# Linear attention's opening: the first head's taps and convolution in halves of the tokens, and the first two steps in an order of their own

## The reference

```python
q = hidden @ Wq; k = hidden @ Wk; v = hidden @ Wv
beta = sigmoid(hidden @ Wb + bb); gate = silu(hidden @ Wg)
q = layernorm(silu(causal_dwconv(q, qconv_w, qconv_b)))   # 4 taps
k = layernorm(silu(causal_dwconv(k, kconv_w, kconv_b)))
# for each token: S = (1 - b) * S + b * v k^T ;  o = S q
out = (o * gate) @ Wo
```

## Time and profile before

| | us |
|---|---|
| median of 3 runs | 1080.46 (1079.77 to 1082.92) |
| the profiled execution, its own time | 1079.62 |
| span of that execution, first to last instruction | 1077.7 |
| first projection of head 0 on TensorE | starts at 390.75 |
| `rows_q(2)`, the first TensorE work of loop step 3 | starts at 459.37 |
| one step after that (`rows_q(3)`) | starts at 481.41 |

### The profile page before, as it was taken

The page is one execution under the profiler, slowest core; times in us unless marked ns, Lnnn a source line. Parts: engine busy times, 40 slices in busy tenths (PEclk is TensorE's granted clock), DMA queues, the critical chain, the costliest instruction groups (busy, mean ns, idle before and its releaser), DMA issues. The chain is left out here.

```text
span 1077.7 us, 19332 instructions
## 1 busy us (share of the span) xinstructions
PE 1020.7 (95%) x6893; PEld 807.8 (75%) x6893; DVE 780.1 (72%) x1645; ACT 676.2 (63%) x1229; POOL 500.4 (46%) x441
## 2 busy tenths in 40 slices
PE   7899999999999986899999999999799999999997
PEld 4333333467888885799899888999699778888997
DVE  5789999646677747889998999989567465333843
ACT  3488888766554447887788787887445353333454
POOL 3252320114079642777767777676406000437443
PEclk9999999999999999899999999999899999999999
DMA  4434443233134203322231122210001113555100
GB/s 96 86 69 65 72 65 62 61 96 102 60 108 109 38 6 114 106 96 64 70 103 64 55 65 87 86 67 23 7 30 40 46 48 100 149 157 170 60 21 20
DMA packets 80794, 79.31 MB, mean 74 GB/s; under 512 B 29384, under 2 KB 67740, under 8 KB 80700
## 3 DMA queue, kind: packets, MB, share of 16 engines
q1 hardware_dynamic: 79968, 77.14, 27.2%
q10 hardware_dynamic: 732, 0.95, 0.3%
HBM read 65.51 MB, written 1.28 MB: 62 GB/s over the span
## 5 line engine op out<-in xcount | busy, mean ns | idle before, releaser
L733 ACT ACTIVATE attn_probs<-attn_rows_k 128x512 f32<-128x512 f32 x256 | 138.9, 595 | 24.4 <-PE attn_rows_k L579 21.2
L579 PE MATMUL attn_rows_k<-attn_q_stack,attn_k_stack 50*128 50x512 f32 x256 | 93.9, 446 | 0.0
L2933 DVE TENSOR_TENSOR late_mids<-late_mids,late_bank 128x512 f32<-128x512 f32 (+1 forms) x50 | 34.4, 688 | 78.3 <-PE late_bank L67 75.3
L842 DVE TENSOR_REDUCE attn_row_max<-attn_rows_q 128x1 f32<-128x1024 f32 x62 | 75.9, 1224 | 11.4 <-PE attn_rows_q L563 5.4
L842 DVE TENSOR_REDUCE attn_row_max<-s_sum 128x1 f32<-128x1024 f32 x62 | 75.7, 1220 | 11.0 <-PE attn_rows_q L563 5.2
L592 PE MATMUL attn_ctx<-attn_probs,attn_v 128*32 128x256 f32 x1024 | 81.5, 391 | 1.6
L65 PE MATMUL late_bank<-net_x_part_low,late_w_T 128*128 128x512 f32 (+1 forms) x192 | 77.9, 406 | 0.0
L66 PE MATMUL late_bank<-net_x_part_low,late_w_T 128*128 128x512 f32 (+1 forms) x192 | 76.1, 396 | 0.0
L67 PE MATMUL late_bank<-net_x_part_low,late_w_T 128*128 128x512 f32 (+1 forms) x192 | 76.0, 396 | 0.0
L1598 POOL TENSOR_TENSOR gold_mids<-gold_mids,s_later 128x512 f32<-128x512 f32 x32 | 53.4, 1705 | 45.5 <-DMA s_later<-gold_weights 43.8
L2838 ACT ACTIVATE late_mids<-late_bank 128x512 f32<-128x512 f32 (+1 forms) x50 | 29.9, 598 | 69.5 <-PE late_bank L67 69.5
(11 more groups left out here) (458 smaller groups left out, 3518.0 us busy)
## 6 DMA issues: line engine op xcount, KB each, us to landing
lin_mix<-decay_sums SPq DMA_DIRECT2D x16, 512.0 KB, 4.1
lin_q_dec<-decay_sums SPq DMA_DIRECT2D x16, 512.0 KB, 5.5
s_later<-gold_weights SPq DMA_DIRECT2D x16, 256.0 KB, 3.8
attn_k_stack<-s_part SPq DMA_DIRECT2D x30, 128.0 KB, 3.5
s_raw_ring<-in_L_ffn_Wg SPq DMA_DIRECT2D x12, 256.0 KB, 2.7
s_raw_ring<-in_L_ffn_Wu SPq DMA_DIRECT2D x12, 256.0 KB, 3.1
attn_k_stack<-s_part SPq DMA_DIRECT2D x33, 64.0 KB, 2.3
gold_raw_w_down<-in_L_ffn_Wd SPq DMA_DIRECT2D x1, 2048.0 KB, 12.0
```

The source lines that it names most:

```text
L579: pe.matmul(out, k_stack[rows, h % SLOTS, t * P:(t + 1) * P], q_stack[rows, h % SLOTS, :], start=True, stop=True).then_inc(scored_k, 1)
L733: act.activation(probs[:, (2 * k + odd) % PB, side * HALF:(side + 1) * HALF], ring_bank(("exped", 4 * k + n + 1)), ACT.Exp).then_inc(exped, 1)
L842: dve.tensor_reduce(row_max[h % 2][:, tile:tile + 1], ps_tile[tile_bank(n)][:, :], axis=AX, op=ALU.max)\
```

## The change

Four things are changed, all in the opening.

1. **Halves.** In head 0 the last tap and the convolution of q and k are made in two halves of the tokens. The first halves of the last tap stand at the end of `act_first`, and the first halves of the convolution on VectorE between `dve_shift` and `dve_low` of the tail of the layer before, and behind it. In `pe_first` the k half is projected ahead of z (the logits of beta).
2. **Order on TensorE.** `rows_q(0)` and `turn_q(0)` move forward; `turn_q(0)` waits no longer for head 1's convolution of q, and `project_q(1)` waits for `q_transposed(0)` instead. `project_gate(0)` moves ahead of `turn_k(0)`.
3. **Order on ScalarE.** The high parts of head 2's weights (`high_q(2)`, `high_k(2)`, `high_v(1)`) and the gate's silu move ahead of `norm_k(0)`.
4. **Order on GpSimd and VectorE.** The low parts of head 2's weights stand ahead of `mask(0)` and `rows_k(0)`; `decay_v(0)` stands behind `power(1, 0)`; `mask(1)` behind `power(1, 1)`. On VectorE the logits follow both convolutions, and head 1's convolutions are exchanged (k first).

SyncE's program is not changed.

```diff
@@ dve_program of the layer before
             tail1.dve_shift(dve, j)
+        linear.first_half_conv(dve, 0)
         for j in (2, 3):
             tail1.dve_low(dve, j)
+        linear.first_half_conv(dve, 1)
@@ pe_first
-        self.project_half(pe, "q", 0, self.pair[3])
+        self.project_half(pe, "q", 0, self.pair[3]).then_inc(self.first_projected, 1)
+        pe.wait_ge(self.k_split, 1)
+        self.project_half(pe, "k", 0, self.pair[1]).then_inc(self.first_projected, 1)
         pe.wait_ge(self.b_split, 1)
         self.project_z(pe, 0)
-        pe.wait_ge(self.k_split, 1)
-        self.project_half(pe, "k", 0, self.pair[1])
@@ pe: turn_q(h), project_q(h)
-            if h + 1 < LH:
+            if 1 <= h < LH - 1:
                 pe.wait_ge(self.q_conved, h + 2)
...
+            if h == 1:
+                pe.wait_ge(self.q_T_done, 1)
@@ pe: the opening's order
         finish_first()
+        rows_q(0)
         project_v(1)
-        rows_q(0)
+        project_k(1)
         sum_decay()
-        project_k(1)
+        turn_q(0)
         rows_k(0)
         project_q(1)
-        turn_q(0)
-        for n in self.STEPS[2:LH + 1]:
+        project_gate(0)
+        turn_k(0)
+        rows_k(1)
+        rows_q(1)
+        score(0)
+        key_values(0)
+        project_q(2)
+        project_k(2)
+        project_v(2)
+        turn_q(1)
+        outputs(0)
+        for n in self.STEPS[3:LH + 1]:
@@ act_first
+        for m, pair in enumerate((3, 1)):
+            act.wait_ge(self.first_projected, m + 1)
+            self.first_tap(act, m, pair, 0, self.first_tapped)
@@ act
         silu(0, 0, self.q_conved, self.q_acted)
+        silu(0, 1, self.k_conved, self.k_acted)
         exp_logit()
         copy_v(1)
         decay_rows()
-        silu(0, 1, self.k_conved, self.k_acted)
+        q_transposed(0)
         tap(1, 1, 1, self.k_projected, self.k_rowed, self.k_tapped)
         high_gate(0)
         tap(1, 0, 3, self.q_projected, self.q_rowed, self.q_tapped)
+        high_q(2)
+        high_k(2)
+        high_v(1)
+        silu_gate(0)
+        silu(1, 1, self.k_conved, self.k_acted)
         norm_k(0)
         silu(1, 0, self.q_conved, self.q_acted)
-        q_transposed(0)
-        silu(1, 1, self.k_conved, self.k_acted)
+        k_transposed(0)
         exp_mix(0)
@@ dve: new, and its use (convolve calls conv_part from HALF for head 0, from 0 for the others)
+    def conv_part(self, dve, h, m, first, last):
+        src = self.pair[(3, 1)[m]]
+        for j in range(TAPS - 1):
+            back = TAPS - 1 - j
+            at = max(first, back)
+            i = dve.scalar_tensor_tensor(self.conv[m][:, at:last], src[:, at - back:last - back], self.taps[:, m, h, j:j + 1],
+                                         self.conv[m][:, at:last], ALU.mult, ALU.add)
+            if j < TAPS - 2:
+                dve.drain()
+        return i
+
+    def first_half_conv(self, dve, m):
+        dve.wait_ge(self.first_tapped, m + 1)
+        self.conv_part(dve, 0, m, 0, HALF)
@@ pool
         power(0, 0, self.q_var, self.q_normed, self.q_rstd)
+        low("gate", self.wg[0], self.g_high, self.g_split, 1)
         power(0, 1, self.k_var, self.k_normed, self.k_rstd)
-        low("gate", self.wg[0], self.g_high, self.g_split, 1)
+        low("q", self.wq[0], self.q_high, self.q_split, 3)
+        low("k", self.wk[0], self.k_high, self.k_split, 3)
+        low("v", self.wv[1], self.v_high, self.v_split, 2)
+        mask(0)
         rows_k(0)
-        mask(0)
         power(1, 0, self.q_var, self.q_normed, self.q_rstd)
-        mask(1)
         pool.sem_clear(range(min(used_numbers), max(used_numbers) + 1))
         decay_v(0)
+        power(1, 1, self.k_var, self.k_normed, self.k_rstd)
+        mask(1)
```

More of the change, by code:

```diff
@@ L1975, in act_first, with first_tap @@
         self.high(act, "q", self.wq[0], self.q_high)
+        self.high(act, "k", self.wk[0], self.k_high)
         self.high(act, "b", self.wb, self.b_high)
-        self.high(act, "k", self.wk[0], self.k_high)
         self.high(act, "v", self.wv[0], self.v_high)
+        for m, pair in enumerate((3, 1)):
+            act.wait_ge(self.first_projected, m + 1)
+            self.first_tap(act, m, pair, 0, self.first_tapped)
+    def first_tap(self, act, m, pair, half, done):
+        cols = slice(half * HALF, (half + 1) * HALF)
+        act.activation(self.conv[m][:, cols], self.pair[pair][:, cols], ACT.Identity, scale=self.taps[:, m, 0, TAPS - 1:TAPS],
+                       bias=self.taps[:, m, 0, TAPS:TAPS + 1]).then_inc(done, 1)
     def act(self, act):
@@ L2073, in act @@
         live = self.live
-        tap(0, 0, 3, self.q_projected, self.q_rowed, self.q_tapped)
+        act.wait_ge(self.q_projected, 1)
+        self.first_tap(act, 0, 3, 1, self.q_tapped)
         high_q(1)
-        tap(0, 1, 1, self.k_projected, self.k_rowed, self.k_tapped)
+        act.wait_ge(self.k_projected, 1)
+        self.first_tap(act, 1, 1, 1, self.k_tapped)
         high_k(1)
@@ L2086, in act @@
         tap(1, 0, 3, self.q_projected, self.q_rowed, self.q_tapped)
+        high_q(2)
[3 more added lines that the diff above has]
+        silu(1, 1, self.k_conved, self.k_acted)
         norm_k(0)
         silu(1, 0, self.q_conved, self.q_acted)
-        q_transposed(0)
-        silu(1, 1, self.k_conved, self.k_acted)
+        k_transposed(0)
         exp_mix(0)
         for n in self.STEPS[2:LH]:
-            if live(n):
+            if live(n) and n > 2:
                 high_q(n)
-            k_transposed(n - 2)
-            if live(n):
+            if n > 2:
+                k_transposed(n - 2)
+            if live(n) and n > 2:
                 high_k(n)
-            silu_gate(n - 2)
-            if n % 2 == 0 and live(n):
+            if n > 2:
+                silu_gate(n - 2)
+            if n % 2 == 0 and live(n) and n > 2:
                 high_v(n // 2)
@@ L2181, in states, with convolve @@
             i.then_inc(self.states_done, 1)
-        def convolve(h, m, pair, tapped, done):
+        def convolve(h, m, tapped, done):
             dve.wait_ge(tapped, h + 1)
[L2185 to L2191, removed]
+            self.conv_part(dve, h, m, HALF if h == 0 else 0, T).then_inc(done, 1)
         def gate(h):
@@ L2220, in dve @@
         live = self.live
-        convolve(0, 0, 3, self.q_tapped, self.q_conved)
+        convolve(0, 0, self.q_tapped, self.q_conved)
+        convolve(0, 1, self.k_tapped, self.k_conved)
         logits()
-        convolve(0, 1, 1, self.k_tapped, self.k_conved)
+        variances(0, 0, 3, self.q_rowed, self.q_rstd, self.q_var)
         decay_logs()
-        variances(0, 0, 3, self.q_rowed, self.q_rstd, self.q_var)
+        norm_q(0)
         mix_biases()
-        norm_q(0)
         variances(0, 1, 2, self.k_rowed, self.k_rstd, self.k_var)
+        convolve(1, 1, self.k_tapped, self.k_conved)
         shift_k(0)
-        convolve(1, 0, 3, self.q_tapped, self.q_conved)
-        convolve(1, 1, 1, self.k_tapped, self.k_conved)
+        convolve(1, 0, self.q_tapped, self.q_conved)
         variances(1, 0, 3, self.q_rowed, self.q_rstd, self.q_var)
@@ L2240, in dve @@
             if live(n):
-                convolve(n, 0, 3, self.q_tapped, self.q_conved)
-                convolve(n, 1, 1, self.k_tapped, self.k_conved)
+                convolve(n, 0, self.q_tapped, self.q_conved)
+                convolve(n, 1, self.k_tapped, self.k_conved)
             gate(n - 2)
```

12 lines of the change are left out of this document (7 added, 5 removed).

## The result

The changed kernel takes 1085.20 us (median of five, 1083.95 to 1086.72), the kernel before 1080.46 (1079.69 to 1082.92) beside it: a ratio of 1.0061, 95% interval 1.0034 to 1.0088. By the medians it is slower by 4.7 us, and 1084.9 was forecast. The ratio is estimated from all runs and is not the quotient of these two medians, which is 1.0044 and lies in its interval; 0.0061 would be 6.6 us. Later runs are given as such ratios, each against runs of the kernel before on the same chip.

What follows compares the result with a forecast made beforehand. TensorE was taken to bound the kernel, so a later `rows_q(2)` carries to the end. 3.6 (`key_values(0)` late) - 0.4 + 1.2 (clock) = 4.4 us on the median 1080.46 gave 1084.9; 8-in-10 range 1080.6 to 1087.2.

Steps and rivals of the forecast that it cites:

- Front part: Opening up to the decay sums: 3.06 us logits' wait gone, yet sums start 0.4 us later, at 416.05.
- the 7.1 us for v, q, k and z: TensorE from 402.2: these four projections take 7.1 us, to 409.2.
- `project_v(1)` 2.95: TensorE behind `rows_q(0)`: this projection takes 2.95 us, as in the profile before.
- The part that decides: ScalarE waits 3.3 us for head 2's weights, `norm_k(0)` ends at 436.2, TensorE waits 9.2, `key_values(0)` starts 3.6 late.
- The term for the clock: From `key_values(0)` to `rows_q(2)`: half clock after a wait of some 5 us adds 1.2 us.
- The 0.4 of gain: After `key_values(0)`: a wait for the low part of head 2's weights disappears, minus 0.4 us.
- The bounds, 0 and 3.4: Limits in us set on the half clock's cost between `key_values(0)` and `rows_q(2)`, taken as 1.2.
- The rival in which it is absorbed: Steady steps: their 0.3 us slack over 13 steps takes up the delay, about 1081.5 us; chance 0.05.
- The table load: ScalarE ahead of the gate's silu: 1.28 us without drain; with 1.38 drain the sum would be 5.8, not 4.4.
- The clock stays up: Rival: no half clock behind TensorE's longer wait, `key_values(0)` 1.0 us late, about 1081.1 us; chance 0.16.
- The weights are there in time: Rival: head 2's weights land by 425.4 for `high_q(2)`, 1077.7 us with the clock up too; chance 0.11.
- It is worse: Rival: 6 us half clock after `key_values(0)` costs 2.7, weights landing 1 us later add 1, 1087.4 us; chance 0.08.

Runs made afterwards that it cites:

- e1: Changed kernel with SyncE issuing head 2's q and k weights and the second pair of v weights ahead of the decay rows' store; ratio to before 1.0021.
- e10: e9 plus 16 unread products on TensorE ahead of `key_values(0)`; ratio to before 1.0018.
- e2: Kernel before with only head 0's taps and convolution in halves and k ahead of z on TensorE, other orders as before; ratio to before 0.9987.
- e7: e2 plus 22 unread products of 512 columns in TensorE's wait ahead of `turn_q(0)`; ratio to before 0.9989.
- e3: Changed kernel without the halves: head 0's taps and convolution whole, z ahead of k, all new orders kept; ratio to before 1.0068.
- e4: Changed kernel plus unread products in TensorE's two long waits, 34 ahead of `turn_k(0)` and 16 ahead of `key_values(0)`; ratio to before 1.0028.
- e9: Changed kernel with the weights issued early as in e1 and `norm_k(0)` ahead of the three high parts on ScalarE; ratio to before 1.0048.
- e5: Changed kernel with e1's early weights and unread products, 22 ahead of `turn_k(0)` and 16 ahead of `key_values(0)`; ratio to before 0.9991, no trace.
- e6: Changed kernel with `decay_v(0)` ahead of `power(1, 0)` on GpSimd; ratio to before 1.0065.

## Why the prediction was right

**The median** came out at 1085.2 where 1084.9 was forecast. Its closeness is partly luck. The sum was made from before's profile and said 4.4 us; the two profiled executions are 7.1 us apart (1079.62 and 1086.72), the medians 4.7. Before's profiled execution lies 0.84 us below its median, the changed one's 1.52 above. This goes with the clock: over the 79 executions of the kernel before that were timed beside e1 to e10, the mean granted clock is 0.993 at the shortest span, 1072.5 us, and 0.974 at the longest, 1088.5 us. The profiled pair has 0.988 and 0.978, the four other runs of the changed kernel 0.979 to 0.982. So the errors found below, 3.5 us in all, are errors against this pair of profiles, and the median doesn't show them whole.

**Front part.** The first product behind the tail's low part started at 402.19 (forecast 402.2), and the half passes took 2.40 us for three, as worked out:

```profile
399.13 2.40 DVE L2170 SCALAR_TENSOR_TENSOR lin_conv_q<-lin_pair,early_lin_taps,lin_conv_q 128x509 f32<-128x509 f32 x3
...
407.37 2.40 DVE L2170 SCALAR_TENSOR_TENSOR lin_conv_q<-lin_pair,early_lin_taps,lin_conv_q 128x512 f32<-128x512 f32 x3 [2.00 <-ACT lin_conv_q L2001]
```

The logits' wait went, as said. But the decay sums started at 419.05, not 416.05. The steps that failed are the 7.1 us for v, q, k and z and "`project_v(1)` 2.95": I had the clock at 1.00 from 402 to 419, and it was at 0.50 from 401.6 to 405.0 and from 411.9 to 415.3. Behind the first, `rows_q(0)` started at 410.95 and not 409.4; under the second `project_v(1)` took 4.5 us (411.80 to 416.26). `project_k(1)` took 2.79, as forecast. This is no accident of one execution: from the product with the low part to the decay sums the forecast had 13.85 us, and all eight profiles with the new order on TensorE have 16.4 to 19.6, while before, e2 and e7 have 13.9 to 14.1. The waits ahead of these falls are short: 1.47, 0.33 and 1.06 (0.7 for the half convolution ahead of `dve_low`) around 400, where before had 1.46, 0.33 and 0.55, and 0.45 and less around 411. That the halves or these waits bring the falls isn't shown. e3, without the halves, had the clock at 0.50 from 407.1 to 413.9, and TensorE had not waited since 400.4. What it did do there, and ahead of the fall at 411.9, is the 24 products of 16 columns for the logits (404.75 to 407.7 in e3, 407.76 to 410.5 in the changed kernel); e2's fall at 396.3 also comes 0.6 us behind these products of its first half. Before has the same products and no fall there, so the cause stays open.

**The part that decides.** Named right in every link, all of it 3 us later than forecast because of the above: ScalarE's wait 4.15 (3.3), `norm_k(0)` ending at 439.1 (436.2), TensorE's wait 10.07 (9.2), half clock behind it, a second wait of 4.64 released by GpSimd (some 5). From the end of `norm_k(0)` to `key_values(0)` it was 11.0 us and not 11.75: the clock was back at 442.6, so `rows_q(1)` ran at full clock, and its statistics started 1.07 us behind its start and not 1.98. `key_values(0)`: 450.07 for 447.95, which is +2.9 and -0.8. By e1 the weights are a cause, worth 4.1 us at `norm_k(0)`, and by e2 and e3 the order is what brings the loss. Not in the prediction was that `shift_k(0)` now stands behind head 1's convolution on VectorE. Here the weights hide this, since `lin_k_shift` was there at 430.1 and the weights at 431.68.

**After `key_values(0)`.** The sum had 15.0 - 0.4 + 1.2 = 15.8 us; it took 17.2. The term for the clock was mis-sized: by e4 it is 1.9, not 1.2 (e10 beside e9 gives 1.2). The 0.4 of gain did not come, since at full clock e4 needs 15.35: in place of the wait for the low part it has one of 0.78 for `lin_normed_q`. The bounds, 0 and 3.4, held. Together: 2.1 and 1.4, so `rows_q(2)` at 467.27 and not 463.8.

**To the end.** From `rows_q(2)` to the end of the span it was 618.3 us before (1077.7 less 459.37) and 617.5 after (1084.8 less 467.27): the delay reached the end but for 0.8 us, and the steps stayed at 22.04. The rival in which it is absorbed is out.

**The table load.** ScalarE's row at 433.06 has a load of 1.28 us and the silu at 434.36, 0.02 behind it. The Trainium skill (ScalarE: Activation LUTs, What ACT_TABLE_LOAD costs) adds 1.38 of drain; here no idle time stands behind the load, so what was taken from rows was right.

**The rivals.** "The clock stays up" didn't happen. e4 keeps it up from 430 on and comes to 1.0028, about half of the loss less, and the prediction's 1081.1, a ratio of 1.0006, is the lower edge of its interval.

"The weights are there in time" was put at 1077.7 with the clock up too, a ratio of 0.9974. e1 has the weights in time and comes to 1.0021; the clock still fell, from 434.1 to 440.9 and again from 447.8 to 454.6. e5 adds the fillers and comes to 0.9991: its interval just reaches the 0.9974, but it is no measurable gain over before, so on that side the prediction probably promised too much.

"It is worse" asked for 6 us of half clock behind `key_values(0)` and for weights 1 us later. In the profiled execution both held, 0.50 from 449.4 to 456.2 and k weights issued at 426.73 that landed 5.4 us later, at 432.1 and not 429.1. What failed there is the price, 2.7 us for the clock where e4 shows 1.9; its 1087.4 is near the profiled execution's 1086.72.

## What to carry to other kernels

Moving a step earlier on an engine that runs its list in order moves its inputs' deadlines too: ask of each step put ahead when its own DMA was issued, and what that issue hangs on. A wait of TensorE that is removed should be followed to its source (here statistics behind ScalarE's sum of work); as long as that is not shorter, another order only gives the wait another place, as e6 and e9 did. And price a new wait with the half clock behind it: here keeping the clock up through two waits gave back 0.0033 of the ratio, nearly as much as the weights' 0.0040. Each of these alone is near the noise, but e5 beside e1 and e10 beside e9 give 0.0030 each for a filler too. Last, don't compare single profiles for less than the 3 us by which the same program differed here.

## What the runs showed that was not expected

- The granted clock fell twice where TensorE had been at most 1.5 us idle at a time (from 401.6 and from 411.9 in the changed kernel, 0.50 for 3.4 us each), and in e3 at 407.1 where it had not waited for 6.7 us, while in the earlier trace rows the first fall came behind a wait of 3.06 us.
- In the idle stretch ahead of `turn_k(0)` (429.1 to 439.2) it fell at 432.3, and it stayed at 0.50 until 442.6, 3.4 us into the work behind that stretch.
- A filled wait doesn't keep the clock up in general: in e4 it did to the end of the opening, in e7 22 products (5.19 us) ahead of `turn_q(0)` (up to 430.5) were followed by a fall at 434.0, behind waits of 0.84 and 1.39.
- A DMA of 128 KB took 5.4 us from issue to landing in the changed kernel as it took 5.3 before, though issued 3 us later.
